# Moving the third group's routing work from the end of the attention part into the first expert tile

## The reference

```python
x = x + jnp.tanh(g_xattn[0]) * xattn(_layernorm(x), ctx_1024, mask, ...)   # 8 batches, 256 queries, 77 keys, 16 heads
x = x + jnp.tanh(g_ffn[0]) * ffn(_layernorm(x), router_w, router_b, w1, w3, w2)
# ffn: logits = x @ router_w + router_b; the best 2 of 4 experts for each of 2048 tokens, with gates that sum to 1
h = silu(x @ w1[e]) * (x @ w3[e])       # 256 -> 1024, for the tokens of expert e
out = gate * (h @ w2[e])                # 1024 -> 256
```

## Time and profile before

| | us |
|---|---|
| median of 3 runs | 481.23 (480.28 to 481.75) |
| the profiled execution, its own time | 479.45 |
| its span | 477.6 |
| PE busy | 458.5 |
| DVE busy | 375.5 |
| ACT busy | 306.8 |
| POOL busy | 199.3 |

### The profile page before, as it was taken

The page is one execution under the profiler, slowest core; times in us unless marked ns, Lnnn a source line. Parts: engine busy times, 40 slices in busy tenths (PEclk is TensorE's granted clock), DMA queues, the critical chain, the costliest instruction groups (busy, mean ns, idle before and its releaser), DMA issues.

```text
span 477.6 us, 11535 instructions
## 1 busy us (share of the span) xinstructions
PE 458.5 (96%) x3720; PEld 432.4 (91%) x3720; DVE 375.5 (79%) x849; ACT 306.8 (64%) x768; POOL 199.3 (42%) x208
## 2 busy tenths in 40 slices
PE   8989999989889999999999999999999999999995
PEld 5768987878778999999999999999999999999894
DVE  1699897869875888886888878888878878887771
ACT  2555564564346766885777757777777776776782
POOL 4669974689882061630245423302302312311312
PEclk9999999999979999999999999999999999999999
DMA  8619998862123112222124222112113102102112
GB/s 252 174 36 364 385 411 345 316 250 76 48 83 97 46 35 57 42 62 35 14 35 90 32 62 47 21 26 47 23 23 45 22 23 34 22 14 35 23 13 24
DMA packets 33824, 45.22 MB, mean 95 GB/s; under 512 B 10211, under 2 KB 30427, under 8 KB 33541
## 3 DMA queue, kind: packets, MB, share of 16 engines
q1 hardware_dynamic: 25999, 35.21, 21.9%
q0 software_dynamic: 6704, 9.04, 11.2%
q10 hardware_dynamic: 1072, 0.35, 0.4%
HBM read 32.92 MB, written 21.82 MB: 115 GB/s over the span
## 4 chain that ended last, share of the span: by engine, by line
PE 62%; DVE 20%; ACT 6%; issue 5%; POOL 3%; DMA 1%; ACTq 1%; DVEq 1%; SPq 0%; POOLq 0%
PE ps_rows L1801 18%; PE ps_wide L1821 6%; PE ps_probT L1801 6%; PE ps_wide L1630 6%; PE ps_misc L1821 6%; DVE w_lo L1439 6%; DVE w_lo L1435 3%; PE ps_misc L1652 3%; PE ps_misc L1581 3%; PE ps_rows L1850 2%; PE ps_probT L1607 2%; DVE ps_rows L1444 2%; DVE hid_lo L1448 2%; ACT hid_hi L1037 2%; PE ps_rows L1595 2%
## 5 line engine op out<-in xcount | busy, mean ns | idle before, releaser
L1265 POOL DMA_INDIRECT out_x<-y_out,meta x35 | 63.9, 1825 | 190.7 <-ACT y_out L1059 185.6
L1439 DVE TENSOR_TENSOR w_lo<-w,w_hi 128x512 fp32r<-128x512 f32 x152 | 104.1, 685 | 13.7 <-issue 6.6
L1801 PE MATMUL ps_rows<-xt_hi,w_hi 128*128 128x256 f32 x384 | 110.7, 288 | 0.2 <-DVE xt_lo L1453 0.2
L1801 PE MATMUL ps_rows<-xt_hi,w_lo 128*128 128x256 f32 x384 | 108.8, 283 | 0.0
L1801 PE MATMUL ps_rows<-xt_lo,w_hi 128*128 128x256 f32 x384 | 108.7, 283 | 0.0
L1008 ACT CAST w_hi<-w 128x512 fp32r x152 | 95.2, 627 | 4.2 <-issue 4.0
L1801 PEld LDWEIGHTS ps_rows<-xt_hi,w_hi 128*128 128x128 f32 x384 | 73.7, 192 | 0.4 <-DVE xt_lo L1453 0.4
L1801 PEld LDWEIGHTS ps_rows<-xt_lo,w_hi 128*128 128x128 f32 x384 | 73.7, 192 | 0.0
L1801 PEld LDWEIGHTS ps_rows<-xt_hi,w_lo 128*128 128x128 f32 x384 | 73.6, 192 | 0.0
L1022 ACT ACTIVATE act_g<-ps_rows 128x256 f32<-128x256 f32 x96 | 37.3, 389 | 30.3 <-PE ps_rows L1801 25.2
L1448 DVE TENSOR_TENSOR hid_lo<-ps_rows,hid_hi 128x256 fp32r<-128x256 f32 x96 | 40.4, 421 | 16.0 <-ACT hid_hi L1037 16.0
(11 more groups left out here) (245 smaller groups left out, 1157.6 us busy)
## 6 DMA issues: line engine op xcount, KB each, us to landing
grouped<-in_pad SPq DMA_DIRECT2D x1, 10296.0 KB
w<-in_L_ffn_w SPq DMA_DIRECT2D x8, 1024.0 KB, 12.1
w2s<-in_L_ffn_w SPq DMA_DIRECT2D x4, 1024.0 KB, 13.7
xg<-grouped SPq DMA_DIRECT2D x16, 256.0 KB, 2.7
out_x<-xall SPq DMA_DIRECT2D x8, 256.0 KB
xall<-in_x SPq DMA_DIRECT2D x1, 1024.0 KB, 12.5
xall<-in_x SPq DMA_DIRECT2D x1, 768.0 KB, 8.1
ctxT<-in_ctx_t SPq DMA_DIRECT2D x2, 308.0 KB, 5.5
```

Of the source, the lines that this page charges most:

```text
L1265: pool.indirect_dma_start(out, bass.IndirectOffsetOnAxis(ap=meta[:, s % 2, t, E:E + 1].bitcast(U32), axis=0), y_out[:, s % 2, t, :], None, ...
L1439: dve.tensor_tensor(w_lo[:, f % NB], unit_weights(e, f), w_hi[:, f % NB].bitcast(F32), ALU.subtract).then_inc(w_lo_done, 1)
L1801: mm = pe.matmul(ps_gu[f % NB][:, m, 0:n], lhs, rhs[:, a, c, 0:n], start=(k == 0), stop=(k % (3 * DC) == 3 * DC - 1), skip_group_check=True)
```

## The change

Of the third group, the norm, the three pieces of transposes, their copies and the router's product leave batch 7 and the stretch behind it and are called in `routing(u)` of slot 0 and slot 1 (norm at u = 0 to 3, pieces at u = 4, 6, 8, copies at 5, 7, 9, product at 10); all that follows from them moves back by 5 to 12 units. The transposes and the product use the bank `ps_route` in place of banks of the scores. In the room between batch 7 and slot 0, PE now runs `up` of units 0 and 1 ahead of `turn_ctx` and `project_o` of batch 7. In POOL's and DVE's bodies of batches 5 and 7 some steps change places.

```diff
@@ ACT: ending(b), routing(u), before run_slots
-                    norm2(act, k, range(0, 2))
-                    turned2_copy(act, k, 0, ps_scores[0][:, 0])
-                    norm2(act, k, range(2, GN))
-                    turned2_copy(act, k, 1, ps_scores[0][:, 1])
-                    weighed_copy(b, 3)
...
+                    if u in (0, 1, 2, 3, 18, 19, 20, 21):
+                        norm2(act, k, (u % 18,))
+                    if u in (5, 7, 9):
+                        turned2_copy(act, k, (u - 5) // 2)
-                    if u in (5, 37):
+                    if u in (16, 37):
...
-                turned2_copy(act, NG - 2, 2, ps_scores[0][:, 0])
                 e = expert_of(act, 0)
                 weights_hi(0, e, 0)
                 x_hi(0, 0)
+                weighed_copy(B - 1, 3)
+                weights_hi(1, e, 1)
                 ctxT_copy(B - 1)
-                for f in range(1, AHEAD):
-                    weights_hi(f, e, f)
+                weights_hi(AHEAD - 1, e, AHEAD - 1)
@@ POOL: body(b)
-                    if b in FINAL:
-                        gates(pool, FINAL[b])
-                        fill(pool, FINAL[b])
                     if not first:
                         context(pool, b - 1, 0)
                     lower(b, 0)
-                    if b in FINAL:
-                        places(pool, FINAL[b])
-                        if last:
-                            scatter(pool, FINAL[b], COPIES[0:1])
+                    if not last:
+                        keys(b + 1, 0)
+                    if b in FINAL:
+                        gates(pool, FINAL[b])
+                        fill(pool, FINAL[b])
                     lower(b, 1)
+                    if last:
+                        places(pool, FINAL[b])
+                        scatter(pool, FINAL[b], COPIES[0:1])
...
                         context(pool, b - 1, 1)
-                    if last:
-                        deviation2(pool, BEGIN[b])
                     lower(b, 2)
                     if b in FINAL and not last:
-                        keys(b + 1, 0)
+                        places(pool, FINAL[b])
...
-                            scatter(pool, FINAL[b], COPIES[1:8])
+                            scatter(pool, FINAL[b], COPIES[1:5])
+                            deviation2(pool, BEGIN[b])
+                            scatter(pool, FINAL[b], COPIES[5:8])
@@ POOL: routing(u): odds 4 -> 14, gates and fill 7 -> 18, places 8 -> 19
-                SCATTER = (9, 10, 15, 16, 18, 23, 24, 25)
+                SCATTER = (20, 22, 23, 24, 25, 26, 28, 30)
@@ DVE: body(b), after body, routing(u)
-                        if s == 0 and b in FINAL:
-                            invert(dve, FINAL[b])
                         if s == 1 and b in BEGIN:
                             variance2(dve, BEGIN[b])
+                        if (b, s) == (B - 1, 2):
+                            invert_sums(b - 1, 1)
                         sink_zeros(b, s)
-                        if s % QT == 0:
+                        if s % QT == 0 and (b, s) != (B - 1, 2):
                             invert_sums(b - 1, s // QT)
                         find_lowest(b, s)
+                        if s == 0 and b in FINAL:
+                            invert(dve, FINAL[b])
...
-                logit(dve, NG - 2, ps_scores[1][:, 0])
+                invert_sums(B - 1, 1)
+                context(dve, B - 1, 1)
                 weights_lo(1, e, 1)
                 residual(B - 1)
                 weights_lo(AHEAD - 1, e, AHEAD - 1)
# routing(u): logit - -> 11, compare 0 -> 12, order_of 1 -> 12, choose 2 -> 13, lag 3 -> 13,
# invert 6 -> 17, hand_out 8, 9, 11, 13 -> 19, 20, 22, 24
@@ PE
-                        turn2(pe, BEGIN[b], 0, ps_scores[0][:, 0])
...
-                turn2(pe, NG - 2, 1, ps_scores[0][:, 1])
-                attend(B - 1, 3, False)
-                turn2(pe, NG - 2, 2, ps_scores[0][:, 0])
...
-                        up(u, f, a, tiles_of(s) * P)
+                        if not (isinstance(u, int) and u < 2):
+                            up(u, f, a, tiles_of(s) * P)
...
-                    if u == 4:
+                    if u in (4, 6, 8):
+                        turn2(pe, NG - 2, (u - 4) // 2)
+                    if u == 10:
+                        route_product(pe, NG - 2)
+                    if u == 15:
                         rank(pe, NG - 2)
...
                 turn_in(0, 0)
-                route_product(pe, NG - 2, ps_scores[1][:, 0])
+                attend(B - 1, 3, False)
+                pe.wait_ge(x_lo_done, 1)
+                up(0, 0, 0, TILE)
                 turn_ctx(B - 1, True)
+                up(1, 1, 0, TILE)
                 project_o(B - 1)
-                pe.wait_ge(lg_copied, NG - 1)
```

More of the change, by code:

```diff
@@ L958, in ending @@
                 def ending(b):
-                    k = BEGIN[b]
                     weighed_copy(b, 0)
@@ L1193, in body @@
                         rsqrt(2)
+                    if b - 1 in FINAL:
+                        scatter(pool, FINAL[b - 1], COPIES[2:4])
+                    if not last:
+                        keys(b + 1, 0)
                     if b in FINAL:
+                        gates(pool, FINAL[b])
+                        fill(pool, FINAL[b])
+                    lower(b, 1)
+                    if last:
                         places(pool, FINAL[b])
-                        if last:
-                            scatter(pool, FINAL[b], COPIES[0:1])
-                    else:
-                        if b - 1 in FINAL:
-                            scatter(pool, FINAL[b - 1], COPIES[2:4])
-                        keys(b + 1, 0)
-                    lower(b, 1)
-                    if b in BEGIN and not last:
+                        scatter(pool, FINAL[b], COPIES[0:1])
+                    elif b in BEGIN:
                         deviation2(pool, BEGIN[b])
@@ L1374, in body @@
                             off_mean(2)
+                        if s == 1 and b in BEGIN:
+                            variance2(dve, BEGIN[b])
+                        if (b, s) == (B - 1, 2):
+                            invert_sums(b - 1, 1)
+                        sink_zeros(b, s)
+                        if s % QT == 0 and (b, s) != (B - 1, 2):
+                            invert_sums(b - 1, s // QT)
+                        find_lowest(b, s)
                         if s == 0 and b in FINAL:
                             invert(dve, FINAL[b])
-                        if s == 1 and b in BEGIN:
-                            variance2(dve, BEGIN[b])
-                        sink_zeros(b, s)
-                        if s % QT == 0:
-                            invert_sums(b - 1, s // QT)
-                        find_lowest(b, s)
                         if s == 0 and b > 1:
@@ L1429, in _ @@
                 hand_out_rest(dve, 1)
-                invert_sums(B - 1, 1)
-                context(dve, B - 1, 1)
                 def w2_lo_of(s, e, q):
@@ L1494, in routing @@
                 def routing(u):
-                    k = NG - 2 if u < 14 else NG - 1
-                    if u == 0:
+                    k = NG - 2 if u < 18 and u != 16 else NG - 1
+                    if u == 11:
+                        logit(dve, k)
+                    if u == 12:
                         compare(dve, k)
-                    if u == 1:
                         order_of(dve, k)
-                    if u == 2:
+                    if u == 13:
                         choose(dve, k)
-                    if u == 3:
                         lag(dve, k)
@@ L1723, in body @@
                         turn_p_end(b, 2, first)
-                    if last:
-                        pe.wait_ge(masked, NS * B)
-                        turn2(pe, BEGIN[b], 0, ps_scores[0][:, 0])
                     attend(b, 2, first)
```

24 lines of the change are left out of this document (11 added, 13 removed).

## The result

The changed kernel takes 483.88 us (median of 4 runs, 483.31 to 484.41), the kernel before 481.15 us beside it (480.28 to 481.75). The ratio is 1.0060 [1.0046, 1.0075]: 2.9 us or 0.6% slower, where 482.0 was forecast, in a range of 479.4 to 484.4, with chances of 0.40 for no clear difference and 0.35 for slower. The profiled execution took 484.41 us with a span of 482.3.

A forecast was written before the change was run, and what follows sets the result against it. PE was taken to bound the kernel, with gains only before 150 us, where it stands still. Terms of -1.6 us, +1.7 and +0.7 for the clock made +0.8, giving 482.0 us, range 479.4 to 484.4.

The forecast's parts named there:

- the one on `L438`: DVE's `invert`, batch 7: the prediction is wrong if this line lasts until 125.5 us.
- rival 2: Batch 7: `invert` starved by POOL, ending after 124.6; `turn_ctx(6)` at 134.4, +2.4 us, 483.6 us; chance 0.20.
- lead at `up(2)`, without what the clock took: PE between batch 7 and slot 0: unit 2 starts 4.4 us earlier, at 148.6 instead of 153.0.
- clock: PE behind its new stops: slow stretches cost 1.7 us at the first, 0.7 together at the two later ones.
- moved product, transposes, late copy: Slots 0 and 1: product and eight transposes add 2.8 us on PE, the copy at u = 9 adds 0.3.
- stop at L365: Fourth group's transposes: PE's stop of 0.3 us vanishes, as PE is 2.8 us later relative to DVE.
- Rival 4: Chain up to 204 us: DVE's queue sets the pace and PE's lead is lost; 0, 481.2 us; chance 0.07.
- PE has no stops there: Slots up to 204 us: argument against DVE's queue setting the pace.
- from 123.85 DVE needs what it needed from 125.31: DVE, batch 7, behind `invert`: the same 3.75 us as before, so strip 1 is found at 127.6.
- I take half, 1.7: Clock behind the 2.45 us stop ahead of `turn_ctx(6)`: half of the bounds 0 to 3.3 us.
- rival 3: Clock falls at each of PE's three stops: +3.5 us, 484.7 us; two falls give +1.8; chance 0.15.
- units 0 and 1 covered this: Ahead of `up(2)`: these units formerly hid the wait for `weights_lo(2)` behind the residual, now a 1.75 us stop.

The follow-up runs named there:

- the run with the filler in the kernel before: The kernel before plus five unread products of 512 columns in PE's stop ahead of `turn_p(7, 1)`: 480.76 us, ratio 0.9978.
- The run with `bias_add` moved: The changed kernel with POOL's `bias_add` for batch 7 moved behind `lower(7, 3)`: 481.52 us, ratio 1.0022.
- the run with the context first: The changed kernel with `places` and the first `scatter` of batch 7 moved behind `lower(7, 3)` on POOL: 480.66 us, ratio 1.0003.
- the filler: The changed kernel plus twelve unread products of 512 columns in PE's stop ahead of `turn_ctx(6)`: 480.19 us, ratio 1.0001.
- the run with the hand-out later: The changed kernel with the third hand-out's four DVE pieces at u = 24 to 27, not 19 to 24: 481.15 us, ratio 1.0017.
- Two pairs of kernels with and without the units ahead: Changed kernel, 1.0060; units 0, 1 back behind `project_o(7)`, 1.0063. Changed kernel with `places`/`scatter`, `bias_add`, residual, hand-out later, 0.9905; units back too, 0.9890.

## Why the prediction was off

The time lies inside the stated range, near its upper end. But the kernel is clearly slower, which the forecast thought a little less likely than no difference, and that the range held owes something to luck: three terms were too low by 1.5 to 1.9 us each, and two that were too high or missing gave 2.1 us back. Of the forecast's own signs of being wrong the one on `L438` was met as it reads: it named 125.5, and `L438` ended at 125.83, which is 125.0 without the early shift and behind rival 2's 124.6 either way.

By its own terms, on the profiled executions, up to the turns of the fourth tile (u = 29), behind which nothing more is lost:

| term | forecast | measured |
|---|---|---|
| lead at `up(2)`, without what the clock took | -4.4 | -2.6 |
| clock | +2.4 | +3.85 |
| moved product, transposes, late copy | +3.1 | +2.4 |
| stop at L365 | -0.3 | +1.6 |
| DVE-paced small stops in slot 1 | 0 | -1.4 |
| sum | +0.8 | +3.85 |

The first measured term is 155.24 - 153.18 = 2.06, less 0.79 (the early shift), less 3.85. The third is 0.33 for the three transposes ahead of the turn at u = 5 and 20.02 - 17.95 = 2.07 between the gathers' turns at u = 5 and 13. With the 0.79 the sum gives the 4.65 us that separate the two traces. The medians are only 2.7 to 2.9 apart. Neither profiled execution is typical: that of before took 479.45 us, 1.7 less than the median of its kernel, and that of after is the slowest of its four and had the lowest mean clock (0.985; 0.988 and 0.989 in the others). The early fall explains the 0.79; that the rest, about 1 us between 3.85 and the medians, is the clock as well is likely, not shown.

The fifth term lies between the turns at u = 13 and u = 21. PE's wait for its weight loads there, in the kernel before, and then the windows of this stretch, before and after:

```profile
PEld ps_misc L1821 <- DVE hid_lo L1448: 0.7, 2, 0.5
PEld ps_wide L1821 <- DVE hid_lo L1448: 0.3, 1, 0.3
```

```profile
180.46:199.65 19.19, 18.76 (x151) 17.98 (x149) 16.78 (x46) 13.50 (x33) 6.14 (x7) 1.00 0.13 38
```

```profile
184.27:202.71 18.44, 18.44 (x160) 18.28 (x159) 16.00 (x50) 12.93 (x32) 6.78 (x12) 1.00 0.06 16
```

After needs 0.75 us less there although it does the rank of the third group as well, which was ahead of the turn at u = 5 before. The rank is worth 0.65: from `up(2)` to that turn 9.33 us passed before with it, and 9.01 after with three transposes (0.33) in its place. So DVE set the pace of this slot before by 1.4 us, in stops of which the list names 1.0. Rival 4 was right in this one slot, and "PE has no stops there" was read too strongly.

**Right.** The stop of batch 5 is gone. `attend(7, 0)` came at 129.31, forecast 128.6 + 0.8. One stop stands ahead of `turn_ctx(6)`, though longer. The stops ahead of `up(0)` and `up(2)` are within 0.25 us. The norms and copies on ACT are hidden, the copy at u = 9 delays nothing, the scatters land in time.

**Wrong, first: "from 123.85 DVE needs what it needed from 125.31".** The forecast left the starvation with `invert` and gave it 1.76 us. What starves is whichever DVE step meets POOL's unbroken run, and that became `sink_zeros(7, 0)`, 3.96 us. The trace of before already had a second such row, on a strip that takes 0.8 when free, and the run with the filler in the kernel before a third, `invert` itself, until `bias_add` ended at 124.72; the forecast had only "one row":

```profile
130.67 2.00 DVE L1352 SCALAR_TENSOR_TENSOR score<-score 128x616 f32<-128x616 f32 x1
```

```profile
121.77 3.00 DVE L438 TENSOR_SCALAR total<-behind 128x4 f32<-128x4 f32 x1 [0.25 <-ACT behind L434]
```

In the changed kernel `L438` ended at 125.83, behind the 124.6 of rival 2, and `turn_ctx(6)` was 1.84 us later than forecast, net of the shift. So rival 2 had the place and nearly the time (483.6), with the wrong instruction. The run with `bias_add` moved shows the cause, 1.8 us; the run with the context first shows the place, 2.7 us.

The Trainium skill ("SBUF — State Buffer", SBUF: two separate sides) says that the port pair of DVE and POOL is locked for one whole instruction while the other side blocks. The traces agree that one side blocks. By that rule alone DVE would get in behind the instruction under way; here it stood behind `lower`, `keys` and `bias_add` in a row, and got in at POOL's pause; without `bias_add` it stood behind `lower` and got in around `keys`, with POOL's pause still to come. The measurement decides; which side goes first when both have an instruction ready is open.

**Wrong, second: "I take half, 1.7" for the clock, and 0.7 for the later stops.** It fell twice on this path, as in rival 3 with two falls, and cost 3.85 us in this execution (2.4 forecast); the filler, which holds up nothing, gives back 2.8 us of the measured time. The bound of 3.3 for the first stop held (2.25), that of the stop ahead of `up(0)`, 1.7, too (1.6).

**Wrong, third: "the stop of 0.3 should vanish".** PE is indeed later relative to DVE, and slot 1 profits by 1.4 us. But the hand-out moved along, from u = 8 to 13 to u = 19 to 24, into the units in which ACT's copy for L365 is due. The step looked at the total of DVE's work and not at what each piece now stands in front of: +1.6 instead of -0.3, which the run with the hand-out later gives back (2.1 us of time).

**Wrong, fourth: "units 0 and 1 covered this", the lead of the units.** Two pairs of kernels with and without the units ahead show no difference that can be measured (1.0060 and 1.0063; 0.9905 and 0.9890). The forecast counted their new stops rightly but had no sum for the old order behind the same late context, where two other stops stand, of 2.0 us together in the one pair and 1.9 in the other, and the clock takes what is gained between them in the first.

## What to carry to other kernels

When steps are reordered on DVE or POOL, don't attach a starved duration to the instruction that showed it. Look for the stretch in which POOL has instructions ready without a break, and ask which DVE step meets it in the new order; then break the run with work that can wait. Moving small steps to later units keeps their sum and changes what they stand in front of: check each against the copy or cast that PE needs next. And cost a stop on PE twice, by itself and by the slow stretch behind it, unless other waits cover that. One profiled execution doesn't fix that second price: the slow stretch comes and goes between executions of the same kernel, so look at the clock of several before a term is read off one.

## What was not expected of the hardware

- A DVE operation stood through several POOL instructions in a row, with nearly the same length in each of six runs (3.95 or 3.96 us, 0.8 when free), and one on 4 columns for 4.24 us (0.15 when free).
- The granted clock fell to 0.50 behind stops of only 0.74 and 0.80 us with work between them (context first), and stayed at 1.00 in the run with the filler in spite of later stops of 1.31, 0.94 and 1.53 us.
- Extra products that nobody reads made the changed kernel 2.8 us faster.
- In four of 14 profiled executions the clock was low for some 3.4 us from 34 us on, in code that is the same in all of them.
